# A vision tower on one core: two sum tables for the experts' output, a router in fewer steps, attention over positions by 128-row products

## The reference

```python
h = tok(x)                                            # patches, layer norm, linear, + b
h = h + attnA(ln(h))      # 12 heads of 16; per image: softmax(q k^T * scale, own position left out but for the first) v; (.) @ w_proj + b_proj
h = h + ffn_block(ln(h))  # attention B, then MLP M; the second half of the images is a sum over three
                          # widths (192, 96, 64 channels, heads likewise) weighted by gumbel_weights
h = h + attnD(ln(h))      # differential attention over the 12 heads of each row
# last: mixture of experts over ln(h)
glog = xf @ Wg + bg       # 4 groups, top 2
elog = xf @ We + be       # 8 experts per group, top 4
gates = softmax(top_k(.)); combine = gw * ew
y = sum over 32 experts e of combine[:, e] * (gelu(xf @ W1[e] + b1[e]) @ W2[e] + b2[e])
h = h + y
```

## Time and profile before

| | us |
|---|---|
| three runs | 922.62, 924.24 (median), 928.3 |
| profiled execution, its own time | 920.78 |
| its span | 918.9 |
| PE busy | 766.5 (83%) |
| expert loop, first L1386 to the end of the last L1394 | 511.98 to 905.4 |
| attention steps of A and of B | 117 to 162 and 174; 226 to 258 and 276 |
| router, group 1 and group 2 | 408 to 439; 456 to 505 |

### The profile page before, as it was taken

The page is one execution under the profiler, slowest core; times in us unless marked ns, Lnnn a source line. Parts: engine busy times, 40 slices in busy tenths (PEclk is TensorE's granted clock), DMA queues, the critical chain, the costliest instruction groups (busy, mean ns, idle before and its releaser), DMA issues.

```text
span 918.9 us, 21916 instructions
## 1 busy us (share of the span) xinstructions
PE 766.5 (83%) x7678; PEld 642.7 (70%) x7678; DVE 391.7 (43%) x1138; ACT 232.7 (25%) x664; POOL 311.5 (34%) x247
## 2 busy tenths in 40 slices
PE   4968889848999964977557799998999999999994
PEld 4964477526756653867534698897989888889893
DVE  4954443242313049975658233333333333333331
ACT  1202211212133211110203233332333323333331
POOL 3833201010001003541210344554545545555554
PEclk9787655857579886987655799999999999999997
DMA  8920000000000002000212266545454645655433
GB/s 194 230 56 1 2 4 3 2 1 3 4 1 1 1 0 104 1 1 1 72 26 98 85 174 169 142 98 142 98 150 96 178 116 143 166 130 144 97 49 71
DMA packets 34628, 70.12 MB, mean 76 GB/s; under 512 B 6422, under 2 KB 20982, under 8 KB 34550
## 3 DMA queue, kind: packets, MB, share of 16 engines
q0 software_dynamic: 15840, 17.71, 12.4%
q10 hardware_dynamic: 8352, 34.30, 10.1%
q1 hardware_dynamic: 10375, 17.22, 7.2%
HBM read 59.23 MB, written 10.76 MB: 76 GB/s over the span
## 4 chain that ended last, share of the span: by engine, by line
PE 34%; DMA 34%; DVE 16%; issue 10%; POOL 2%; ACT 1%; POOLq 1%; SPq 1%; DVEq 0%
DMA summed<-arena,number_u 33%; PE bank L1174 4%; PE bank L1194 3%; PE bank L1140 2%; DVE arena L1039 2%; PE bank L1213 2%; DVE arena L1036 2%; PE bank L1249 2%; PE bank L1265 2%; PE bank L1289 2%; PE bank L1231 2%; PE bank L1182 1%; PE bank L1242 1%; PE bank L1232 1%; PE bank L1152 1%
## 5 line engine op out<-in xcount | busy, mean ns | idle before, releaser
L590 POOL DMA_INDIRECT summed<-arena,number_u x80 | 127.0, 1587 | 148.3 <-DMA summed<-arena,number_u 134.9
L745 ACT ACTIVATE arena<-bank,arena 128x128 f32<-128x128 f32 x234 | 64.8, 376 | 126.6 <-PE bank L1389 126.6
L584 POOL DMA_INDIRECT arena<-normed_rows,fetch_u x80 | 78.7, 983 | 41.3 <-issue 21.9
L1394 PE MATMUL bank<-arena 128*128 128x192 f32 x468 | 84.0, 328 | 7.8 <-DVE arena L1123 6.8
L1394 PEld LDWEIGHTS bank<-arena 128*128 128x128 f32 x468 | 75.3, 190 | 10.6 <-issue 10.4
L526 POOL TENSOR_SCALAR rstd<-mv 128x4 f32<-128x4 f32 x12 | 2.8, 230 | 213.8 <-DVE mv L812 213.8
L1103 DVE COPY arena<-bank 128x256 f32<-128x256 f32 x81 | 34.4, 425 | 92.0 <-PE bank L1371 74.7
L537 POOL TENSOR_TENSOR arena<-arena,v_space 128x2304 f32<-128x2304 f32 x8 | 34.5, 4319 | 111.9 <-DVE arena L1054 111.9
L1121 DVE COPY number_u<-table_u x80 | 12.3, 154 | 136.2 <-DMA summed<-arena,number_u 135.0
L1386 PE MATMUL bank<-arena 128*128 128x128 f32 x468 | 59.7, 277 | 1.2 <-issue 0.7
L1386 PEld LDWEIGHTS bank<-arena 128*128 128x128 f32 x468 | 56.6, 191 | 4.3 <-issue 4.0
(11 more groups left out here) (228 smaller groups left out, 1386.9 us busy)
## 6 DMA issues: line engine op xcount, KB each, us to landing
arena<-in_moe_w_dram ACTq DMA_DIRECT2D x15, 579.0 KB
arena<-in_moe_w_dram ACTq DMA_DIRECT2D x15, 576.0 KB
w_space<-in_moe_w_dram ACTq DMA_DIRECT2D x7, 579.0 KB
w2small<-in_moe_w_dram ACTq DMA_DIRECT2D x7, 579.0 KB
w_space<-in_moe_w_dram ACTq DMA_DIRECT2D x7, 576.0 KB
wab<-in_moe_w_dram ACTq DMA_DIRECT2D x7, 576.0 KB
arena<-in_xf_dram SPq DMA_DIRECT2D x8, 480.0 KB, 14.1
arena<-in_w_dram SPq DMA_DIRECT2D x8, 450.0 KB, 12.1
```

The lines of the kernel that those rows point to most:

```text
L584: pool.indirect_dma_start(out=mo_stage[:, s * ROWN:(s + 1) * ROWN], out_offset=None, in_=normed_rows, in_offset=bass.IndirectOffsetOnAxis( ...
L590: pool.indirect_dma_start(out=summed, out_offset=bass.IndirectOffsetOnAxis(ap=number_u[:, s:s + 1], axis=0), in_=mo_res[:, s * D:(s + 1) * ...
L745: nc.scalar.activation(mo_hT[:, m, :], bank[2 + m][:, 0:P], ACT.Gelu, bias=b1[:, m:m + 1]).then_inc(free[2 + m], 1)
L1394: ins = mm(bank[0][:, 0:D], mo_hT[:, m, :], w2e[:, m, :], start=(m == 0), stop=(m == MC - 1))
```

## The change

Four edits, independent of each other:

1. **Two sum tables.** Even tiles add into `summed[0]`, odd ones into `summed[1]`, so an add waits for the add before the last only. That wait now stands at the top of POOL's step, and a semaphore (`result_free`) tells DVE. SP fills the second table with zeros first. At the end SP copies the first table to `out`, and POOL then adds the second one to `out` by an accumulating DMA of 4096-byte pieces.
2. **Router.** The four tiles' logits go into one bank, the bias is added by DVE in the copies, and a comparison is a subtraction and one `is_ge` against a table that holds 0 or the smallest float: two wide operations for four. E's choice comes first, then G's, then the two softmaxes. `begin` of group 1 moves from behind group 2's gates to right behind group 1's slots.
3. **Attention A and B.** `ptbd` spans eight images (128x1536), V is stored spread so that two heads take 32 columns, and 12 products of 128 rows by 32 weight columns by 128 columns write `oT` itself: no `osb`, no transposes of it, steps of depth two rather than three.
4. **Biases.** No one-row products but one: the biases are added to the residual by POOL (24 additions of 128x192), A's value bias folded through the output weights first (step `bias`, two products in bank 7 ahead of the first qk). Seven loads of small tensors become eleven. fc2 of the small half runs its widths in another order, after all its gelus.

```diff
-        + attn("A", 0, 2) + [("front", "A", 1)] + attn("A", 2, 3) + [("back", "A", 1)] + attn("A", 3, 7)
...
+        + attn("A", 0, 2) + [("front", "A", 1)] + attn("A", 2, 3) + [("back", "A", 1)] + attn("A", 3, 6)
...
-        + last(2, 7) + [("norm", "R", 0)] + last(7, 8) + [("gates", "R", 0)] + last(8, 9) + [("slots", "R", 0)]
-        + last(9, T + 3) + [("norm", "R", 1), ("gates", "R", 1), ("begin", "R", 0), ("slots", "R", 1), ("counts", "R", 0), ("begin", "R", 1), ("table", "R", 0)])
+        + last(2, 7) + [("norm", "R", 0)] + last(7, 8) + [("gates", "R", 0)] + last(8, 9) + [("slots", "R", 0), ("begin", "R", 0)]
+        + last(9, T + 3) + [("norm", "R", 1), ("gates", "R", 1), ("slots", "R", 1), ("counts", "R", 0), ("begin", "R", 1), ("table", "R", 0)])
...
-            sp.wait_ge(sem("accumulated"), total * 16 + ACC0)
-            sp.dma_start(out[:, :], summed[0:TOK, :]).then_inc(sem("out_stored"), 16)
+            pairs = sp.value_load(starts[0:1, NE + 1:NE + 2], min_val=1, max_val=MAXT // 2)
+            sp.wait_ge(sem("accumulated0"), pairs * 16 + 16)
+            sp.dma_start(out[:, :], summed[0][0:TOK, :]).then_inc(sem("out_begun"), 16)
+            sp.wait_ge(sem("out_begun"), 16)
...
+            def clear_values():
+                for t in range(T):
+                    filled(pool, "tok", t)
+                nc.gpsimd.memset(spread_v, 0.0).then_inc(sem("values_clear"), 1)
...
+                for t in range(4 * n, 4 * n + 4):
+                    pool.wait_ge(sem(f"normed_{L}"), t + 1)
+                    nc.gpsimd.tensor_tensor(out=res[:, t, :], in0=res[:, t, :], in1=by[:], op=ALU.add).then_inc(sem(f"biased_{L}"), 1)
...
-                    added, result = pool.snap(i * 16 + ACC0), pool.snap(i + (moe_base[0] + 1))
+                    added, result = pool.snap(pair * 16 + 16), pool.snap(i + (moe_base[0] + 1))
+                    pool.wait_ge(sem(f"accumulated{s}"), added)
+                    pool.sem_inc(sem("result_free"), 1)
...
-                    pool.wait_ge(sem("accumulated"), added)
-                    pool.sem_inc(sem("adding"), 1)
-                    pool.indirect_dma_start(out=summed, out_offset=bass.IndirectOffsetOnAxis(ap=number_u[:, s:s + 1], axis=0),
-                                            in_=mo_res[:, s * D:(s + 1) * D], in_offset=None, compute_op=ALU.add).then_inc(sem("accumulated"), 16)
+                    pool.indirect_dma_start(out=summed[s], out_offset=bass.IndirectOffsetOnAxis(ap=number_u[:, s:s + 1], axis=0),
+                                            in_=mo_res[:, s * D:(s + 1) * D], in_offset=None, compute_op=ALU.add).then_inc(sem(f"accumulated{s}"), 16)
+            pool.wait_ge(sem("out_begun"), 16)
+            pool.wait_ge(sem("accumulated1"), pool.snap(pairs * 16 + 16))
+            pool.sem_inc(sem("adding"), 1)
+            pool.dma_start(out=out.rearrange("(p t) d -> p (t d)", p=P), in_=summed[1][0:TOK, :].rearrange("(p t) d -> p (t d)", p=P),
+                           accum_op=ALU.add, max_dma_last_dim=6 * D * 4).then_inc(sem("out_stored"), 16)
+            pool.wait_ge(sem("out_stored"), 16)
...
-                    nc.scalar.activation(V[:, t, :], ps[:, 0:D], ACT.Copy).then_inc(free_of(L, "V", t), 1)
+                    v = ps[:, 0:D].rearrange("p (h q x) -> p h q x", q=2, x=HD)
+                    if L == "A" and t == 0:
+                        act.wait_ge(sem("values_clear"), 1)
+                    nc.scalar.activation(spread_v[:, t, :, 0, 0:HD], v[:, :, 0, :], ACT.Copy)
+                    nc.scalar.activation(spread_v[:, t, :, 1, HD:2 * HD], v[:, :, 1, :], ACT.Copy).then_inc(free_of(L, "V", t), 1)
...
-                    tt(out=ptbd[t % 2], in0=repeat(src, 2, QB),
+                    tt(out=ptbd[t % 2], in0=repeat(src, 2, TB),
                        in1=repeat(repeat(blockmask[:], 1, H), 3, NTOK), op=ALU.mult).then_inc(free_of(L, "PT", t), 1)
-                if t >= 3:
-                    ps = filled(dve, L, "proj", t - 3)
-                    tt(out=res[:, t - 3, :], in0=ps[:, 0:D], in1=res[:, t - 3, :], op=ALU.add).then_inc(free_of(L, "proj", t - 3), 1)
+                if t >= 2:
+                    q = t - 2
+                    dve.wait_ge(sem(f"biased_{L}"), q + 1)
...
-            def top_gates(which, lg, R, n, k, order):
+            def choose_top(which, lg, R, n, k):
                 a4 = cmpa[:, 0:R * n * n].rearrange("p (r a b) -> p r a b", a=n, b=n)
-                b4 = cmpb[:, 0:R * n * n].rearrange("p (r a b) -> p r a b", a=n, b=n)
                 other, own = repeat(lg, 2, n), repeat(lg, 3, n)
-                link(tt(out=a4, in0=other, in1=own, op=ALU.is_gt))
-                link(tt(out=b4, in0=other, in1=own, op=ALU.is_equal))
-                low = tri[:].rearrange("p (a b) -> p a b", b=E)[:, 0:n, 0:n]
-                link(tt(out=b4, in0=b4, in1=repeat(low, 1, R), op=ALU.mult))
-                link(tt(out=a4, in0=a4, in1=b4, op=ALU.add))
                 chosen, d, mx = gview(which, "sel"), gview(which, "d"), gview(which, "mx")
+                link(nc.vector.reduce_max(mx, lg, AX_X))
+                tt(out=d, in0=lg, in1=repeat(mx, 2, n), op=ALU.subtract).then_inc(sem("gate_shifted"), 1)
+                link(tt(out=a4, in0=other, in1=own, op=ALU.subtract))
+                least = tri[:].rearrange("p (a b) -> p a b", b=E)[:, 0:n, 0:n]
+                link(tt(out=a4, in0=a4, in1=repeat(least, 1, R), op=ALU.is_ge))
...
-                for t in range(t0, t1):
-                    ps = filled(dve, "logit", t)
-                    nc.vector.tensor_copy(lgG[:, t - t0, :], ps[:, 0:G])
-                    nc.vector.tensor_copy(lgE[:, (t - t0) * G:(t - t0 + 1) * G, :], ps[:, G:G + NE].rearrange("p (g e) -> p g e", g=G)).then_inc(free_of("logit", t), 1)
-                was_read(dve, "logit", t1 - 2)
-                was_read(dve, "logit", t1 - 1)
-                top_gates("G", lgG, R, G, KG, 2 * g + 1)
-                top_gates("E", lgE, R * G, E, KE, 2 * g + 2)
+                ps = filled(dve, "logit", g)
+                lg = ps[:, 0:R * (G + NE)].rearrange("p (r e) -> p r e", r=R)
+                tt(out=lgG[:, 0:R, :], in0=lg[:, :, 0:G], in1=repeat(route[:, 0:G], 1, R), op=ALU.add)
+                tt(out=lgE.rearrange("p (r g) e -> p r (g e)", r=R), in0=lg[:, :, G:G + NE], in1=repeat(route[:, G:G + NE], 1, R), op=ALU.add).then_inc(free_of("logit", g), 1)
+                was_read(dve, "logit", g)
+                choose_top("E", lgE, R * G, E, KE)
+                choose_top("G", lgG, R, G, KG)
+                top_gates("E", R * G, E, 2 * g + 1)
+                top_gates("G", R, G, 2 * g + 2)
...
-                    dve.wait_ge(sem("accumulated"), added)
+                    dve.wait_ge(sem("result_free"), added)
...
-                    ps = claim(L, "AV", q)
+                    ps = claim(L, "oT", q)
                     for hh in range(H):
-                        for r in range(0, P, QUAD):
-                            ins = mm(ps[r:r + QUAD, hh * HD:(hh + 1) * HD], ptbd[q % 2][r:r + QUAD, hh, :, :].rearrange("p b i -> p (b i)"),
-                                     V[r:r + QUAD, q, hh * HD:(hh + 1) * HD], start=True, stop=True)
-                    ins.then_inc(full_of(L, "AV", q), 1)
+                        f, r = hh // HH, hh % HH // 2 * QUAD
+                        ins = mm(ps[r:r + QUAD, f * P:(f + 1) * P], spread_v[:, q, hh // 2, hh % 2, :], ptbd[q % 2][:, hh, :, :].rearrange("p b i -> p (b i)"),
+                                 start=(hh % 2 == 0), stop=(hh % 2 == 1))
+                    ins.then_inc(full_of(L, "oT", q), 1)
...
-                        mm(ps[:, 0:D], oT[:, q % 2, k, :], wo[:, k, :], start=(k == 0), stop=False)
-                    mm(ps[:, 0:D], ones[0:1, :], row("boutA" if L == "A" else "boutB" if q < T // 2 else "boutS"), start=False, stop=True).then_inc(full_of(L, "proj", q), 1)
+                        ins = mm(ps[:, 0:D], oT[:, q % 2, k, :], wo[:, k, :], start=(k == 0), stop=(k == 1))
+                    ins.then_inc(full_of(L, "proj", q), 1)
```

192 lines of the change are left out of this document (108 added, 84 removed).

## The result

The changed kernel takes 888.42 us (median of four runs, 887.76 to 893.14) against 924.99 in the same comparison: ratio 0.9624, 95% interval 0.958 to 0.9668. The forecast was 902 with a range of 868 to 918, faster at 0.85. Direction and range hold; the likeliest case's own range (890 to 912) just misses.

What follows compares the result with a forecast made beforehand. PE was taken as the bound in attention, DVE's chain in the router, adds level with PE in the loop. 920.8 - 16 + 2 - 18 - 4 - 2.5 + 16 = 898.3; with 3.4, 902 us, range 868 to 918.

Steps and rivals of the forecast that it cites:

- likeliest case: Whole kernel: the forecast's own case, 902 us with a range of 890 to 912, chance 0.42.
- Expert loop: Expert tiles: with two tables the waits for adds go and PE is next latest, -16 us.
- End: After the last tile: last add 3.1 us earlier, accumulating DMA of 9.5 us for a copy of 4.7, +2 us.
- Router, group 2: Router's second group: logits back to back -6.6 us, less wait for place counts as `begin` moves away -3.9.
- Router, group 1: Router's first group: fewer wide operations, exponentials' wait filled by E's choice, -7.5 us; `begin` costs nothing there.
- router gains little: Router rival: ACT stays behind PE or `begin` now blocks PE's D steps, +14 us, 916 us, chance 0.07.
- Biases: Bias products dropped: -4 us in fc2, -2.5 for A's value bias; POOL's additions and clearing hidden.
- Attention: Attention A and B: 12 products per block replace AV, oT and bias products go, +16 us, clock mostly 0.50.
- 19 units of 24: Attention block: 24 instructions overlap only at 5 changes of column group, 4.05 us at half clock, 2.05 at full.
- hidden behind PE's 6: Attention step: DVE's block diagonal of 1.8 us runs behind some 6 us of PE work.
- the rivals: Attention: clock up to 1.00, 874 us, chance 0.26; three column groups side by side, 869 us, chance 0.05.
- the rival with drains: Attention: each change of column group drains the array, 16 blocks +85 us, 985 us, chance 0.06.

Runs made afterwards that it cites:

- experiment 2: The kernel before with only the two sum tables added (zeros, both waits and the merge as in the change): 919.16 us, ratio 0.9954 to the kernel before.
- experiment 8: The kernel of experiment 3 run once more, unchanged, on another chip: 888.27 us, ratio 0.9577 to the kernel before.
- experiment 12: The changed kernel with the last transfer a plain copy to the output, leaving out the first table's part of the sum: ratio 0.9601 to the kernel before.
- experiment 3: The changed kernel with `begin` of group 1 put back behind group 2's gates: 880.48 us, ratio 0.9511 to the kernel before.
- experiment 4: The changed kernel with `begin` of group 1 between group 2's gates and its slots: 882.2 us, ratio 0.9518 to the kernel before.
- experiment 11: The changed kernel with POOL's clearing of the spread V moved earlier, to the first half's token step: 887.42 us, ratio 0.959 to the kernel before.
- experiment 5: The changed kernel with the four products of one column group in a row: 905.58 us, ratio 0.9729 to the kernel before.
- experiment 6: The changed kernel with the 12 products in turn over the three column groups: 895.45 us, ratio 0.9591 to the kernel before.
- experiment 7: The changed kernel with the 12 products on the first 32 rows only: A's first transposes to B's first qk took 44.1 us for 43.2.
- Experiment 9: The changed kernel with DVE's block diagonal made for four of eight images only: A's stretch took 38.8 us for 43.2, B's 52.3 for 54.3.

## Why the prediction was right, and where it was wrong

*Expert loop: mechanism right, size not settled.* -18.4 for -16 in the two profiles, by the mechanism named: no wait for adds, tiles 4.53 to 4.54 us apart where nothing is loaded. Of the 18.4, 14.5 us are idle time of PE that went (12.1 with the tables alone, experiment 2): these the tables gave. The other 4.0 are PE's busy time, 372.2 to 368.2 for the same products. They lie beyond the upper bound of 16.7 that I had named, and since two executions of one program differ by 4.8 us in that figure (experiment 8), they are not shown to be the edit's. Timed alone, the tables were worth 1 to 8 us, with an end longer by 4.0 us in the profile, so 5 to 12 in the loop: the term of 16 was too large by some 4 us at the least, though the changed kernel's profile seems to bear it out.

*End: the right sign, +4.4 for +2.* The end of the changed kernel:

```profile
868.56 0.61 SPq L453 DMA_DIRECT2D out_dram<-summed  x1
869.55 1.59 POOL L612 DMA_INDIRECT summed<-arena,number_u  x1 [0.36 <-issue]
874.97 0.99 POOL L617 DMA_DIRECT2D out_dram<-summed  x1 [3.83 <-DMA summed<-arena,number_u]
```

and its transfers:

```profile
out_dram<-summed SPq DMA_DIRECT2D x1, 768.0 KB, 5.3
out_dram<-summed POOLq DMA_DIRECT2D x1, 768.0 KB, 7.3
```

The last add starts 3.1 us earlier against the last tile's start, as forecast. The accumulating DMA took 7.3 us, not 9.5, nearer to 4.7 as expected of large pieces. I missed two things. The last add runs beside SP's copy of the other table: it took 5.4 us from 869.55 to 874.97, where it had been 3.5. And from there to the end of the span it is 10.7 us, where SP's copy had 5.1. With the plain copy of experiment 12, issued by POOL too, it is 8.2: so some 2.5 us are the accumulation, and 3.1 come with a transfer issued by POOL in pieces of 4096 bytes; what they consist of is not shown.

*Router, group 2: about right,* -10.8 for -10.5, of which 2.7 belong to the place of `begin` (experiment 3 has -8.2); PE now waits for DVE's gates there and no longer the other way round:

```profile
464.71 0.80 PE L1361 MATMUL bank<-arena,ones 128*128 128x128 f32 x2 [10.89 <-DVE arena L997]
```

*Router, group 1: wrong sign, +3.5 for -7.5.* The failed step is "it costs nothing in its new place if PE is idle there, which it was". The gates did come early, by 9.2 us at the place counts (from 33.4 us behind the router's first transposes to 24.1). But `begin` waits for ACT, and PE is in order: what is queued behind it is the last step of attention over heads. I looked at whether PE was idle, not at who comes behind the waiting instruction. It is the rival "router gains little", in its second form ("`begin` now blocks PE's D steps"), for group 1; experiments 3 and 4 show it, 14.4 and 14.5 us. With `begin` at its old place the router's two stretches gain 10.9 and 8.2 us, where the terms without the move were 7.5 and 6.6: these were rather too small, and the move, priced at -3.9, cost 11.7 net.

*Biases: half right.* fc2 of the small half is 2.7 us shorter for four bias products; of the large half's gain most turned into a wait for DVE (1.8), and fc1 of the small half took 1.7 us longer at a granted clock of 0.76 for 0.82, so that from fc2's first product to the router it was 1.8 us in all for -4. Up to A's first transposes the kernel is 1.7 us later, for -2.5. Its first qk starts at 81.4 us for 73.6; POOL's clearing held DVE for 2.4 us on the way (experiment 11), and the rest, with the `bias` step that waits for the last token tile, was not taken apart. In nine other profiles the same code took 117.5 to 122.8 us to that point (117.3 before, 119.1 in the changed kernel's profile), so the size is not settled, but none shows the -2.5.

*Attention: wrong, -11.7 for +16* (A's first transposes to fc2's first product, 158.4 us before and 146.7 after; 143.9 to 146.9 in six other profiles with the same attention). Two steps failed. The first is "neighbours on different parts of the array run together", hence 19 units of 24: the block takes 1.94 at half clock and 1.10 at full, not 4.05 and 2.05, a factor of 2.3 to 2.6 under one by one. L1389 has groups that alternate at every instruction, and I read the limit of that row as PE's; experiments 5 and 6 show that the overlap reaches over four instructions of a group. The Trainium skill's figure that I set aside, 2.38 for three tiles of 32 columns, there with 512 columns streamed ("TensorE: Matmul & The Clock Gate", "Packing small matmuls"), is near what the trace shows: 2.55 / 1.10 = 2.3 with the last one's drain. It doesn't cover the order of experiment 5, 2.55 / 1.99 = 1.3. 14 blocks of 1.94 for 4.05 are -29.5, which takes the +16 to -13.5. The second is the clock. "A product on a quarter of the array does not hold the clock, and 128 rows by 32 columns are a quarter too" put 32 rows by 128 columns and 128 rows by 32 columns down as alike; the granted clock was 0.69 and 0.76, and with a quarter of the rows, all else the same, 0.53 and 0.50 (experiment 7). Behind both stands "hidden behind PE's 6": DVE took PE's place as the bound, so that neither the clock nor a shorter block was worth what the rivals gave (874 and 869). The rows that show it:

```profile
150.47 1.25 DVE L869 TENSOR_SCALAR zx<-h,mv,rstd 128x192 f32<-128x192 f32 x4 [1.47 <-POOL rstd L526]
151.64 1.75 DVE L907 TENSOR_TENSOR arena<-bank,blockmask 128x1536 f32<-128x1536 f32 x1
...
153.44 1.95 PE L1257 MATMUL bank<-arena 128*32 128x128 f32 x24 [4.34 <-DVE arena L907]
```

PE's block waits 4.34 us for DVE's block diagonal, which stands behind a norm that waits for POOL. The waits of the block for the block diagonal from 60 to 300 us, in the changed kernel and in the kernel before:

```profile
PE bank L1257 <- DVE arena L907: 15.2, 6, 4.9
```

```profile
PE bank L1213 <- DVE arena L871: 2.0, 4, 0.6
```

The 1.8 us of DVE (1.75 measured) were to be hidden behind 6 us of PE; these 6 were not there to hide them. Experiment 9 shows DVE's part in A; in B it stays argued.

So the total was in range because a term of 21 us too high and one of 11 us too low met, beside three that came out about right, one of them (the loop) with help from the execution. That is luck: the mechanism was right for the adds and the gates, wrong for attention and for `begin`.

Two slips in the prediction's arithmetic changed nothing else. The chances for "faster" sum to 0.41 + 0.31 + 0.08 = 0.80, not 0.82, so 0.83 would have been stated for 0.85. And the rival with drains counts 12 changes of column group per block, where the order has 5.

## What to carry to other kernels

Before a step is moved on an in-order engine, look at what is queued behind it, not only whether the engine is idle at that place: here 14 us. Take the same program's profile twice before a difference of a few us between two stages is put down to an edit: here 6.7 us in the loop and 2 us in an attention stretch came without one. Price a block of small products with both its own time and the time of the engine that feeds it; where PE gets faster by packing, the block diagonal that the packing needs can set the pace. And an order in which a group of columns gets eight instructions in a row throws away most of the packing that four or two in a row give.

## What the runs showed of the hardware that I had not expected

- Instructions on three groups of 32 columns run side by side at 2.3 to 2.4 times the speed estimated for one by one (2.55 us), with up to four in a row to a group (1.10 us), much less with eight (1.99); a change of group has no cost of its own (1.08 with 11 changes).
- With 32 rows in use for 128, all else the same, the granted clock stayed at 0.50 to 0.53 for 0.69 to 0.76.
- A memset on POOL, which reads nothing, held a DVE operation with one input for its whole length, 2.60 us for 0.17, in both places where it was put.
- The same program's expert loop took 370.8 and 377.5 us in two executions on two chips, at the same granted clock of 0.99.
- One transfer of 768 KB took 5.1 us from issue to the end of the span as SP's copy, 8.2 as POOL's copy in pieces of 4096 bytes and 10.7 as POOL's accumulation in the same pieces.
